# A two-phase attention and mixture-of-experts kernel on one core: lambda and bias set-up moved, the last second layers reordered, unread matmuls added on TensorE

## The chip, the core and the metric

The kernel runs on one core of one Trainium2 chip. The metric is the device time of one execution in microseconds (us); the time of the kernel before is the median of three runs. Engines are called as the profile calls them: PE is TensorE's matmul stream and PEld its weight loads, DVE is VectorE, ACT is ScalarE, POOL is GpSimd, SP is SyncE, which issues most DMAs.

## What is computed

The input is 8192 tokens of width 256. Phase 1 is a differential attention over the heads of one token (not over the sequence), with a residual:

```
x1 = x + ((attn1 - lam*attn2) * rms * ln_w + ln_b) * (1 - LAMBDA_INIT) @ Wo      # heads of layernorm(x)
lam = exp(sum(lq1*lk1)) - exp(sum(lq2*lk2)) + LAMBDA_INIT
scores = softmax(layernorm(x1) @ w_gate); top 2 of 8 experts, capacity 1024 rows each
out = x1 + sum over the 2 experts of weight * ((silu(a) * g) @ c_proj[e]),  [a, g] = row @ c_fc[e]
```

Phase 2 is the experts' part: each expert has up to 1024 rows, 256 wide, a first layer to 2 x 384 and a second layer back to 256. `ln_b` is not zero, so its contribution through Wo is a row of 256 numbers, the same for every token: the bias row.

## The kernel before

Every engine has its own program, in order, and semaphores join them.

**Phase 1** goes over 64 tiles of 128 tokens. Each engine runs steps i = 0, 1, 2, ..., and in a step it handles one stage each of several tiles. DVE in step i: `score_subtract` (L993) of tile i-1, `prob_difference` (L1012, gives w_att) of i-2, `score_products` (L972) of tile i, `prob_sum` (L1000) of i-1, `score_sum` (L979) of i, `prob_normalise` (L1005) of i-1, `score_max` (L986) of i, `scale_a` (L1020) of i-3, and every fourth tile the gating's small operations. ACT makes copies, exponentials and logarithms (xT L489, k_sb L494, x1 L570, aT_sq L552, aT_ln L557, p_ln/p_rec L543/L546). POOL multiplies attention weights with V in `head_products` (L238, one instruction of 2048 columns a tile) and issues two indirect DMAs a tile that scatter the token's row into a table in HBM sorted by expert (L419). PE in step i: `project_qk` (L762) of tile i-2, `sum_heads` (L785, 16 transposes that add up the heads) of i-6, `project_v` (L773) of i-3, `mean_squares` (L792) of i-6, `out_project` (L801 to L808) of i-7, `transpose_x` (L752) of i. `project_qk(t)` waits for DVE's products of tile t-2, `sum_heads(t)` for POOL's products of tile t.

Set-up work sits between these steps. In step 0 DVE centres the weights (L914, L918), then does `lambda_terms` (L924 to L928; it waits for the last small weight loads), then `score_products(0)`. ACT takes the exponentials of lambda in step 2 (L471). PE makes the bias row in PSUM in step 5 (L738). DVE, in step 3, splits the row into three bf16 parts whose sum is the f32 value, in nine dependent instructions of 265 columns (`bias_split`, L949 to L958), and places part j in row j of `bias_parts`. `out_project` then adds the bias with one bf16 matmul of ones by `bias_parts` (L801); the first `out_project` waits for it. The constants are made by POOL at the start; the semaphore `consts` goes to 1 when the identity matrix and a few others are ready.

At the end of phase 1 POOL issues the scatters of the last tiles one after the other. When all have landed, SP loads the first chunk of the table (`xe`, L343).

**Phase 2** goes over 16 chunks of 512 rows, two for each expert; steps are called m. In step m PE does, for j = 0, 1, 2, a third of the first layer of chunk m-1 (L872: 12 matmuls of 512 columns), after the first of them the eight transposes that take in chunk m (L863), and then the whole second layer of chunk m-2 (L883: 36 matmuls of 256 columns, for each 128 rows k nine matmuls; it waits until all three thirds j of the hidden layer are there). f32 numbers are split into a high and a low part, made by ACT and DVE (x_hi L658, x_lo L1217, silu L663, hidden L1222, h_hi L670, h_lo L1226). The second layer's result is scaled by ACT (`scale_output`, y_sb L679) and added to the output by POOL with one indirect DMA for each 128 rows (L451), four for each chunk. In step 16, and only there, the second layer of chunk 14 stands after the last third of the first layer of chunk 15:

```
def second_layer_after(m):
    return NHT - 1 if isinstance(m, int) and m == CHUNKS else 0
```

Step 17 is the second layer of chunk 15 alone.

Of the kernel before, what the change touches and what calls it, by code (L numbers as in the profile page):

```python
# [6 lines left out]
P = 128  # L7
# [38 lines left out]
def build_block(nc, x, wq, wk, wv, wo, lq1, lk1, lq2, lk2, ln_w, ln_b, w_gate, c_fc, c_proj, out):  # L46
# [11 lines left out]
    with ExitStack() as ctx:  # L58
# [27 lines left out]
        with ExitStack() as first:  # L86
# [14 lines left out]
            bias_h = [one(f"bias_h{j}", [P, E + AUX], BF16) for j in range(3)]  # L101
            bias_r = [one(f"bias_r{j}", [P, E + AUX]) for j in range(2)]
            bias_s = [one(f"bias_s{j}", [P, E + AUX]) for j in range(2)]
# [84 lines left out]
        wo_scaled = sem("wo_scaled")  # L188
# [88 lines left out]

        def second_layer_after(m):
            return NHT - 1 if isinstance(m, int) and m == CHUNKS else 0
# [82 lines left out]
        def _(pool):  # L362
# [35 lines left out]
            chain(pool.memset(g_before[0][:, :], 0.0))  # L398
            chain(pool.memset(rows[:, :, :], 0.0))
# [5 lines left out]
            pool.nop().then_inc(consts, 1)  # L405

# [17 lines left out]
            def step(i):  # L424
                if live(i - 11):
                    scatter(i - 11)
                if 0 <= i < LAST_V:
                    head_products(pool, i)

# [35 lines left out]
        def _(act):  # L465
# [135 lines left out]
            def step(i):  # L601
# [28 lines left out]
                if live(i):  # L630
                    copy_xT(i)
                if live(i - 3):
# [49 lines left out]
            def chunk_step(m, v, turn):  # L682
# [4 lines left out]
                for j, q in tiles:  # L687
# [6 lines left out]
                    if j == second_layer_after(m) and chunk_live(m, 2):  # L694
# [5 lines left out]
        def _(pe):  # L700
            pe.wait_ge(consts, 1)

# [153 lines left out]
            pe.wait_ge(slot_ready, NG)  # L856

# [29 lines left out]

            def chunk_step(m, v, turn):
                b0, b1, b2 = v % 2, (v - 1) % 2, (v - 2) % 2
                wb1, wb2 = ((v - 1) // NCH) % 2, ((v - 2) // NCH) % 2  # L890
                for j in range(NHT):
# [16 lines left out]
        def _(dve):  # L908
# [27 lines left out]

            def bias_split():

                n = 0

                def after(ins):
                    nonlocal n
                    n += 1
                    ins.then_inc(bias_chain, 1)
                    dve.wait_ge(bias_chain, n)

                dve.wait_ge(consts, 2)
                dve.wait_ge(bias_done, 1)
                after(nc.vector.tensor_copy(bias_f[:, :], bank_wo[:, 0:E + AUX]))  # L949
# [318 lines left out]
```

## Time and profile before

| | us |
|---|---|
| median of 3 runs | 696.95 (695.79 to 697.55) |
| the profiled execution | 695.95 |
| its span, first to last instruction | 694.1 |
| phase 1, to the last scatter's issue | about 0 to 453 |
| phase 2 | about 454 to 694 |
| mean granted TensorE clock | 0.969 of full |

The rows below are from that one execution. A timeline row gives the start, the time taken, the engine and line, the operation with the tile that it writes and those that it reads, the number of instructions merged in it, and in brackets how long the engine had been idle and what ended that. A granted clock of 1.00 is 2.4 GHz, 0.50 is 1.2 GHz.

### The profile page before, as it was taken

The page shows a single profiled execution, that of the slowest core. Times are in us where ns is not written, and L with a number is a line of the kernel's source. Part 1 is how long each engine was busy: PE and PEld are TensorE (multiplying, and loading weights), DVE is VectorE, ACT ScalarE, POOL GpSimd, SP SyncE. Part 2 cuts the span into 40 slices and gives each one's busy share as a digit, 9 for nine tenths or more (in the row PEclk, how much of TensorE's full clock was granted, in tenths as well). Part 3 has the DMA queues.
Part 4 walks back from the last instruction along what each step waited for, and adds up shares of the span by engine and source line. Part 5 has one row for each costly group of instructions (what it writes and reads, how often), then busy time and mean ns, then how long its engine had stood idle before and what let it go on. Part 6 is the DMA issues. An engine that isn't in the chain of part 4 may idle for free. (4 is left out here: it accounts for less than half of the span.)

```text
span 694.1 us, 12873 instructions
## 1 busy us (share of the span) xinstructions
PE 634.8 (91%) x3644; PEld 507.8 (73%) x3644; DVE 529.8 (76%) x1202; ACT 487.3 (70%) x1692; POOL 512.1 (74%) x294
## 2 busy tenths in 40 slices
PE   6889999999999999999999997049999999999990
PEld 3567777777777777777777776048898898889880
DVE  3999999999999999999999997214455456455430
ACT  3568889888988998898899888425455455465440
POOL 4446688898899889889989887734567566676534
PEclk9999999999999999999999999559999999999996
DMA  7991113223222322211201001133565664764434
GB/s 197 346 358 42 32 63 108 64 77 109 82 74 93 106 74 71 92 48 31 63 2 32 31 1 32 32 95 106 78 140 111 132 139 77 160 139 67 69 32 51
DMA packets 57836, 63.43 MB, mean 91 GB/s; under 512 B 7449, under 2 KB 53630, under 8 KB 57776
## 3 DMA queue, kind: packets, MB, share of 16 engines
q1 hardware_dynamic: 42416, 45.66, 20.6%
q0 software_dynamic: 15360, 17.08, 14.2%
q8 instruction: 24, 0.39, 0.3%
q14 instruction: 36, 0.29, 0.1%
HBM read 27.57 MB, written 43.78 MB: 103 GB/s over the span
## 5 line engine op out<-in xcount | busy, mean ns | idle before, releaser
L238 POOL TENSOR_TENSOR v_prod<-w_att,v_sb 128x2048 f32<-128x2048 f32 x62 | 233.0, 3759 | 50.4 <-DVE w_att L1012 47.2
L419 POOL DMA_INDIRECT slot_table<-rows,g_slot x128 | 129.1, 1009 | 32.0 <-issue 30.6
L451 POOL DMA_INDIRECT out_dram<-y_sb,e_tok x64 | 99.6, 1557 | 65.3 <-ACT y_sb L679 50.8
L979 DVE TENSOR_REDUCE bank_s<-qk_prod 128x128 f32<-128x2048 f32 x64 | 146.1, 2282 | 0.0
L972 DVE TENSOR_TENSOR qk_prod<-bank_qk,k_sb 128x2048 f32<-128x2048 f32 x64 | 145.8, 2279 | 0.0
L785 PEld LDWEIGHTS bank_a<-ident,v_prod 128*128 128x128 f32 x1024 | 115.5, 141 | 33.8 <-issue 30.4
L762 PE MATMUL bank_qk<-wqkv,xT 128*128 128x512 f32 x256 | 120.7, 594 | 4.7 <-DVE qk_prod L972 4.7
L785 PE MATMUL bank_a<-ident,v_prod 128*128 128x128 f32 x1024 | 122.3, 273 | 1.0 <-POOL v_prod L238 1.0
L762 PEld LDWEIGHTS bank_qk<-wqkv,xT 128*128 128x128 f32 x256 | 43.7, 190 | 36.2 <-issue 36.2
L773 PE MATMUL bank_v<-wqkv,xT 128*128 128x265 f32 x256 | 69.3, 393 | 0.0
L670 ACT CAST h_hi<-hidden 128x512 fp32r<-128x512 f32 x48 | 29.9, 622 | 55.8 <-DVE hidden L1222 55.8
L808 PE MATMUL bank_wo<-wo_s,aT_n 128*128 128x265 f32 x256 | 67.9, 387 | 0.0
L438 POOL TENSOR_TENSOR w_lo<-w,w_hi 128x1536 fp32r<-128x1536 f32 (+1 forms) x16 | 43.0, 2709 | 25.9 <-ACT w_hi L649 25.9
L1226 DVE TENSOR_TENSOR h_lo<-hidden,h_hi 128x512 fp32r<-128x512 f32 x48 | 33.5, 699 | 22.8 <-ACT h_hi L670 22.8
L773 PEld LDWEIGHTS bank_v<-wqkv,xT 128*128 128x128 f32 x256 | 43.7, 190 | 4.7
L808 PEld LDWEIGHTS bank_wo<-wo_s,aT_n 128*128 128x128 f32 x256 | 43.8, 191 | 4.2
L792 PE MATMUL bank_a<-aT_sq,head_ones 128*128 128x256 f32 x128 | 38.6, 383 | 5.3 <-ACT aT_sq L552 5.3
L580 ACT ACTIVATE rows<-x_ring,neg_mr,rstd 128x256 f32<-128x256 f32 x64 | 38.4, 600 | 5.3
L552 ACT ACTIVATE aT_sq<-bank_a 128x256 f32<-128x256 f32 x64 | 24.5, 382 | 22.2 <-PE bank_a L785 22.2
L1222 DVE TENSOR_TENSOR hidden<-silu,bank_a 128x512 f32<-128x512 f32 x24 | 16.4, 684 | 27.7 <-ACT silu L663 27.6
L1222 DVE TENSOR_TENSOR hidden<-silu,bank_qk 128x512 f32<-128x512 f32 x24 | 16.5, 687 | 25.4 <-ACT silu L663 25.2
L1212 DVE CAST e_tok<-xe 128x4 int32<-128x4 f32 x16 | 16.9, 1056 | 24.5 <-DMA out_dram<-y_sb,e_tok 24.5
(168 smaller groups left out, 1417.5 us busy)
## 6 DMA issues: line engine op xcount, KB each, us to landing
slot_table<-fill SPq DMA_DIRECT2D x8, 1056.0 KB, 13.1
xe<-slot_table SPq DMA_DIRECT2D x16, 528.0 KB, 3.7
out_dram<-x_ring SPq DMA_DIRECT2D x16, 512.0 KB, 3.0
x_ring<-in_L_attn_x_dram SPq DMA_DIRECT2D x15, 512.0 KB, 3.6
w<-in_L_ffn_c_fc_dram SPq DMA_DIRECT2D x8, 768.0 KB, 5.1
w<-in_L_ffn_c_proj_dram SPq DMA_DIRECT2D x8, 384.0 KB, 5.7
slot_table<-rows,g_slot POOLq DMA_INDIRECT x128, 2.5
out_dram<-fill SPq DMA_DIRECT2D x1, 1024.0 KB, 13.5
```

Source lines behind the costliest of these rows:

```text
L238: eng.tensor_tensor(v_prod[b][:, :, :].rearrange("p m (n e) -> p m n e", n=H), w_att[b][:, :, :].rearrange("p n m -> p m n").unsqueeze(3). ...
L419: pool.indirect_dma_start(out=table, out_offset=bass.IndirectOffsetOnAxis(ap=g_slot[g % SLOT_BUFS][:, j, k:k + 1], axis=0), in_=rows[:, r, ...
L438: pool.tensor_tensor(lo[b][:, :, :].rearrange("p k n -> p (k n)"), w[b][:, :, :].rearrange("p k n -> p (k n)"), hi[b][:, :, :].rearrange(" ...
L451: pool.indirect_dma_start(out=out, out_offset=bass.IndirectOffsetOnAxis(ap=e_tok[n % 2][:, k:k + 1], axis=0), in_=y_sb[n % 2][:, k, :], in ...
L580: nc.scalar.activation(rows[:, r, 0:E], x_ring[:, u, 0:E], ACT.Identity, bias=neg_mr[:, u:u + 1], scale=rstd[:, u:u + 1]).then_inc(xn2_rea ...
L762: last = nc.tensor.matmul(bank_qk[b][:, :, :].rearrange("p a e -> p (a e)"), xT[t % XT][:, k, :], wqkv[:, k, 0:2 * E], start=(k == 0), sto ...
L773: last = nc.tensor.matmul(bank_v[:, 0:E + AUX], xT[t % XT][:, k, :], wqkv[:, k, 2 * E:], start=(k == 0), stop=(k == 1))
L785: last = nc.tensor.matmul(bank_a[b][:, k * P:(k + 1) * P], v_prod[b][:, m, k * P:(k + 1) * P], ident[:, :], is_transpose=True, start=(m == ...
L792: nc.tensor.matmul(bank_a[b][:, E:], head_ones[:, :], aT_sq[b][:, :], start=True, stop=True).then_inc(ms_done, 1)
L808: last = nc.tensor.matmul(bank_wo[:, 0:E + AUX], aT_n[b][:, k * P:(k + 1) * P], wo_s[:, k, :], start=False, stop=(k == 1), skip_group_chec ...
L972: nc.vector.tensor_tensor(qk_prod[b][:, :].rearrange("p (n m f) -> p n m f", n=H, m=H), q4, k4, ALU.mult).then_inc(qk_multiplied, 1)
L979: nc.vector.tensor_reduce(scores[b].rearrange("p (c s) -> p s c", c=2), qk_prod[b][:, :].rearrange("p (s c d) -> p s c d", c=2, d=D), AX_X ...
```

## The change

- `lambda_terms` moves on DVE from ahead of `score_products(0)` to behind `score_sum(0)`; its exponentials move on ACT from step 2 to step 4.
- The bias row is copied from PSUM by ACT (`copy_bias`, step 5, behind `copy_xT(5)`), and the split moves from DVE to POOL, where it stands behind `head_products(0)` and so ahead of `head_products(1)`. It becomes seven instructions: the three parts are put into rows 0, 32 and 64 of `bias_parts` by copies of one partition each, the rest of which is cleared at the start.
- PE issues five matmuls of the identity by itself, 128 columns, ahead of its first wait for weights, and thirty of them between the phases, behind a wait for the scatters of tile 61. Nothing reads their result.
- In step 16 the second layer of chunk 14 stands after the first third, as in other steps. The second layer of chunk 15 is reordered: j is the outer loop, so that the parts of j = 0 and 1 need only the first two thirds of the hidden layer.

```diff
@@ gpsimd @@
+            chain(pool.memset(bias_parts[:, :], 0.0))
...
+            def bias_split():
...
+                pool.wait_ge(bias_copied, 1)
+                after(pool.tensor_copy(bias_h[0][:, :], bias_f[:, :]))
+                after(pool.tensor_tensor(bias_r[0][:, :], bias_f[:, :], bias_h[0][:, :], ALU.subtract))
+                after(pool.tensor_copy(bias_h[1][:, :], bias_r[0][:, :]))
+                after(pool.tensor_tensor(bias_r[1][:, :], bias_r[0][:, :], bias_h[1][:, :], ALU.subtract))
+                after(pool.tensor_copy(bias_parts[0:1, :], bias_h[0][0:1, :]))
+                after(pool.tensor_copy(bias_parts[32:33, :], bias_h[1][32:33, :]))
+                pool.tensor_copy(bias_parts[64:65, :], bias_r[1][64:65, :]).then_inc(bias_ready, 1)
+                pool.wait_ge(bias_ready, 1)
...
                 if 0 <= i < LAST_V:
                     head_products(pool, i)
+                if i == 0:
+                    bias_split()
@@ scalar @@
+            def copy_bias():
+                act.wait_ge(bias_done, 1)
+                nc.scalar.copy(bias_f[:, :], bank_wo[:, 0:E + AUX]).then_inc(bias_copied, 1)
...
-                if i == 2:
-                    lambda_exps()
...
                 if i == 4:
+                    lambda_exps()
                     copy_gate()
...
                     copy_xT(i)
+                if i == 5:
+                    copy_bias()
...
-                    if j == second_layer_after(m) and chunk_live(m, 2):
+                    if j == 0 and chunk_live(m, 2):
                         scale_output(m - 2, b2)
@@ tensor @@
             pe.wait_ge(consts, 1)
+            def keep_going():
+
+                nc.tensor.matmul(bank_v[:, 0:P], ident[:, :], ident[:, :], start=True, stop=True)
+
+            for _ in range(5):
+                keep_going()
...
             pe.wait_ge(slot_ready, NG)
+            pe.wait_ge(scattered[(NT - 3) % ROWS], 32 * ((NT - 3) // ROWS + 1))
+            for _ in range(30):
+                keep_going()
...
+            def last_second_layer(n, b, wb):
+
+                for j in range(NHT):
+                    past(pe, h_lo_ready, n * NHT + j)
+                    for k in range(CB):
+                        if j == 0 and k % 2 == 0:
+                            past(pe, y_scaled, n * CB + k + 1, CB)
+                        parts = ((h_lo, w2_hi), (h_hi, w2_lo), (h_hi, w2_hi))
+                        for i, (h, w) in enumerate(parts):
+                            last = nc.tensor.matmul(p2_y[k // 2][:, (k % 2) * E:(k % 2 + 1) * E], h[b][:, j, k * P:(k + 1) * P], w[wb][:, j, :],
...
+                        if j == NHT - 1 and k % 2 == 1:
+                            last.then_inc(y_done, 1)
...
-                    if j == second_layer_after(m) and chunk_live(m, 2):
-                        past(pe, h_lo_ready, (m - 2) * NHT + NHT - 1)
+                    if j == 0 and chunk_live(m, 2):
                         past(pe, w_lo_ready, expert_of(v, turn, 2) * 2 + 1)
-                        second_layer(m - 2, b2, wb2)
+                        if isinstance(m, int) and m == CHUNKS + 1:
+                            last_second_layer(m - 2, b2, wb2)
+                        else:
+                            past(pe, h_lo_ready, (m - 2) * NHT + NHT - 1)
+                            second_layer(m - 2, b2, wb2)
@@ vector @@
-            def bias_split():
...
-                if i == 3:
-                    bias_split()
                 if i == 0:
                     centre_weights()
-                    lambda_terms()
...
                 if live(i):
                     score_sum(i)
                 if i == 0:
                     numbers_of_experts()
+                    lambda_terms()
```

## Rows read from the trace of the kernel before

**Rows 1.** Busy time in one stretch of phase 1: engines, then clock, DMA share, GB/s

```profile
220.00:260.00 40.00, 40.00 (x226) 30.02 (x225) 39.89 (x105) 36.14 (x145) 35.98 (x20) 1.00 0.25 85
```

**Rows 2.** Timeline of the start, PE, ACT and DVE

```profile
4.44 3.75 PE L707 MATMUL bank_qk<-w_raw,mean_w 128*128 128x512 f32 x4 [4.44 <-DMA w_raw<-in_L_attn_Wk_dram]
...
11.68 0.38 ACT L494 ACTIVATE k_sb<-bank_qk 128x256 f32<-128x256 f32 x1 [1.35 <-PE bank_qk L762]
...
14.00 0.19 DVE L924 TENSOR_TENSOR lam_prod<-lam_in 128x32 f32<-128x32 f32 x1 [3.55 <-DMA lnwb<-in_L_attn_ln_b_dram]
...
14.33 2.28 DVE L972 TENSOR_TENSOR qk_prod<-bank_qk,k_sb 128x2048 f32<-128x2048 f32 x1
...
30.62 0.35 ACT L489 COPY xT<-bank_t 128x256 f32<-128x256 f32 x1
```

**Rows 3.** Timeline around the bias split on DVE, and PE's wait behind it

```profile
35.48 0.42 DVE L949 COPY bias_f<-bank_wo 128x265 f32<-128x265 f32 x1
...
39.97 0.28 DVE L993 TENSOR_TENSOR s_sub<-bank_s,s_max 128x128 f32<-128x128 f32 x1
...
41.00 0.70 PE L792 MATMUL bank_a<-aT_sq,head_ones 128*128 128x256 f32 x2 [3.08 <-ACT aT_sq L552]
```

**Rows 4.** Timeline between the phases: tile 61's last scatter, first chunk

```profile
447.04 0.97 POOL L419 DMA_INDIRECT slot_table<-rows,g_slot  x1 [0.30 <-issue]
...
458.43 1.09 PE L863 MATMUL bank_t<-ident,xe 128*128 128x128 f32 x4 [18.79 <-DMA xe<-slot_table]
...
461.81 1.19 PE L872 MATMUL bank_qk<-x_hi,w_lo 128*128 128x512 f32 x2 [1.45 <-ACT x_hi L658]
...
466.72 0.60 PE L863 MATMUL bank_t<-ident,xe 128*128 128x128 f32 x4
```

**Rows 5.** The chain that ended last, in order of time

```profile
452.16 2.06 DMA slot_table<-rows,g_slot
...
663.20 2.72 PE bank_qk L872 x12
...
671.04 2.16 PE bank_a L883 x18
```

**Rows 6.** Timeline of the end, chunks 14 and 15

```profile
660.52 0.60 ACT L663 ACTIVATE silu<-bank_qk 128x512 f32<-128x512 f32 x1 [0.74 <-PE bank_qk L872]
...
662.52 0.69 DVE L1226 TENSOR_TENSOR h_lo<-hidden,h_hi 128x512 fp32r<-128x512 f32 x1 [0.69 <-ACT h_hi L670]
...
668.50 0.53 PEld L883 LDWEIGHTS bank_wo<-w_hi,h_lo 128*128 128x128 f32 x3
...
672.42 1.55 POOL L451 DMA_INDIRECT out_dram<-y_sb,e_tok  x1 [9.76 <-ACT y_sb L679]
...
679.83 1.55 POOL L451 DMA_INDIRECT out_dram<-y_sb,e_tok  x1 [0.30 <-issue]
```

**Rows 7.** Stretches around PE's pauses: busy times, granted clock, DMA share, GB/s

```profile
36.00:40.00 4.00, 1.92 (x14) 1.44 (x12) 3.75 (x12) 0.16 (x1) 0.00 (x0) 1.00 1.09 335
...
434.00:436.00 2.00, 0.00 (x0) 0.00 (x0) 1.11 (x13) 1.94 (x11) 1.45 (x2) 0.89 0.27 86
...
465.00:466.00 1.00, 1.00 (x4) 0.81 (x3) 0.00 (x0) 0.00 (x0) 0.00 (x0) 0.50 0.58 207
```

**Rows 8.** POOL's elementwise groups by form: busy us, mean ns, idle before

```profile
L238 POOL TENSOR_TENSOR v_prod<-w_att,v_sb 128x2048 f32<-128x2048 f32 x62 | 233.0, 3759 | 50.4 <-DVE w_att L1012 47.2 <-ACT v_sb L530 2.0
...
L438 POOL TENSOR_TENSOR w_lo<-w,w_hi 128x1536 fp32r<-128x1536 f32 x8 | 28.1, 3507 | 25.9 <-ACT w_hi L649 25.9
L438 POOL TENSOR_TENSOR w_lo<-w,w_hi 128x768 fp32r<-128x768 f32 x8 | 15.3, 1911 | 0.0
```

**Rows 9.** Timeline of tile 0 from POOL's products to PE, and project_qk(5)

```profile
25.56 3.75 POOL L238 TENSOR_TENSOR v_prod<-w_att,v_sb 128x2048 f32<-128x2048 f32 x1 [16.94 <-DVE w_att L1012]
...
32.25 0.59 PE L792 MATMUL bank_a<-aT_sq,head_ones 128*128 128x256 f32 x2
...
33.32 1.95 PE L762 MATMUL bank_qk<-wqkv,xT 128*128 128x512 f32 x4 [0.26 <-DVE qk_prod L972]
```

More of the change, by code:

```diff
@@ L100, in build_block @@
             bias_f = one("bias_f", [P, E + AUX])
-            bias_h = [one(f"bias_h{j}", [P, E + AUX], BF16) for j in range(3)]
+            bias_h = [one(f"bias_h{j}", [P, E + AUX], BF16) for j in range(2)]
             bias_r = [one(f"bias_r{j}", [P, E + AUX]) for j in range(2)]
-            bias_s = [one(f"bias_s{j}", [P, E + AUX]) for j in range(2)]
             bias_parts = one("bias_parts", [P, E + AUX], BF16)
@@ L187, in build_block @@
             sem(n) for n in "wo_transposed woT_copied gate_folded gate_copied bias_done bias_ready".split())
-        wo_scaled = sem("wo_scaled")
+        wo_scaled, bias_copied = sem("wo_scaled"), sem("bias_copied")
         x_transposed, xT_copied, qk_done, v_done, k_copied, aux_copied, v_copied = (
@@ L276, in chunk_live @@
             return not isinstance(m, int) or 0 <= m - lag < CHUNKS
-        def second_layer_after(m):
-            return NHT - 1 if isinstance(m, int) and m == CHUNKS else 0
         def expert_of(v, turn, lag):
@@ L405, in _, with after @@
             pool.nop().then_inc(consts, 1)
+            def bias_split():
+                n = 0
+                def after(ins):
+                    nonlocal n
+                    n += 1
+                    ins.then_inc(bias_chain, 1)
+                    pool.wait_ge(bias_chain, n)
+                pool.wait_ge(bias_copied, 1)
[7 more added lines that the diff above has]
+                pool.wait_ge(bias_ready, 1)
             def scatter(t):
@@ L886, in second_layer @@
                         last.then_inc(y_done, 1)
+            def last_second_layer(n, b, wb):
[7 more added lines that the diff above has]
+                            last = nc.tensor.matmul(p2_y[k // 2][:, (k % 2) * E:(k % 2 + 1) * E], h[b][:, j, k * P:(k + 1) * P], w[wb][:, j, :],
+                                                    start=(j == 0 and k % 2 == 0 and i == 0), stop=(j == NHT - 1 and i == len(parts) - 1),
+                                                    skip_group_check=True)
+                        if j == NHT - 1 and k % 2 == 1:
+                            last.then_inc(y_done, 1)
             def chunk_step(m, v, turn):
@@ L935, in lambda_difference @@
                 dve.wait_ge(lam_chain, 4)
-            def bias_split():
[L939 to L949, printed above, removed]
-                after(nc.vector.tensor_copy(bias_h[0][:, :], bias_f[:, :]))
-                after(nc.vector.tensor_tensor(bias_r[0][:, :], bias_f[:, :], bias_h[0][:, :], ALU.subtract))
-                after(nc.vector.tensor_copy(bias_h[1][:, :], bias_r[0][:, :]))
-                after(nc.vector.tensor_tensor(bias_r[1][:, :], bias_r[0][:, :], bias_h[1][:, :], ALU.subtract))
-                after(nc.vector.tensor_copy(bias_h[2][:, :], bias_r[1][:, :]))
-                after(nc.vector.tensor_scalar(bias_s[0][:, :], bias_h[0][:, :], ident[:, 0:1], None, ALU.mult))
-                after(nc.vector.scalar_tensor_tensor(out=bias_s[1][:, :], in0=bias_h[1][:, :], scalar=ident[:, 1:2], in1=bias_s[0][:, :],
-                                                     op0=ALU.mult, op1=ALU.add))
-                nc.vector.scalar_tensor_tensor(out=bias_parts[:, :], in0=bias_h[2][:, :], scalar=ident[:, 2:3], in1=bias_s[1][:, :],
-                                               op0=ALU.mult, op1=ALU.add).then_inc(bias_ready, 1)
             def numbers_of_experts():
```

## The prediction

> **What bounds the kernel now.** I read the busy times by stretch first, then the timelines of the start, of the change between the phases and of the end. In the middle of phase 1 both PE and DVE work without a pause, 40.00 and 39.89 of 40 us [rows 1]; POOL and ACT have some 4 us left. So phase 1 is as long as the one of the two whose unbroken run begins too late. DVE's run begins at 14.33 [rows 2]. PE's begins at 41.00, after 3.08 us of waiting [rows 3]: DVE split the bias from 35.48, so its s_sub came only at 39.97, ACT's exponential of it and the squares behind it stood in the queue, and `mean_squares(1)` waited for these. From there on PE issues the same instructions whatever the change does, so **phase 1 ends earlier by as much as `mean_squares(1)` does, and no more**. What DVE saves beyond that it gives back waiting for PE.
>
> Between the phases POOL's scatters lead, then one load; the granted clock has fallen to half, and PE's first third of a layer takes 461.81 to 466.72, 4.91 us [rows 4], where one at full clock takes 2.72 [rows 5]. At the end POOL leads: the four output scatters of chunk 15 start at 679.83 [rows 6] and all behind them is fixed.
>
> **Lambda.** DVE waited 3.55 us for the small loads although k_sb was done at 11.68 + 0.38 = 12.06. It can begin the products at 12.1. The four small instructions, 14.33 - 14.00 = 0.33, return behind `score_sum(0)`, where the loads have long landed. Gain for DVE 14.33 - 12.1 - 0.33 = 1.9 us [rows 2]. The exponentials in ACT's step 4 are one small instruction in a queue that waits for DVE: nothing, and if that cover is gone, its own 0.2 us (an estimate from DVE's 0.19 for an instruction of like size).
>
> **Five matmuls at the start.** PE's four passes of 512 columns run at 0.85 us each, 3.75 with the last one's tail [rows 2], the half clock. In rows 4 PE worked from 461.81 on, and the clock was still 0.50 in 465 to 466 [rows 7] and full soon after, say 4.4 us after the work began. An identity matmul of 128 columns is two passes of a quarter of 0.85, so five take 2.1 us, from about 2.1 (when the identity is made) to 4.3: done when the weights come at 4.44 [rows 2]. If the clock then rises at 2.1 + 4.4 = 6.5, the last one and a half passes take half as long: 0.65 us. Bounds: 0 (it rises as before) to 1.7 (all four passes at full clock). DVE's total lead is then 2.5 us.
>
> **Bias split.** DVE loses its nine instructions, about 3.75 us, and the pause of PE that they caused. But POOL gets seven, in front of `head_products(1)`. The copy on ACT stands behind xT(5), which was at 30.62 [rows 2] and hangs on DVE's sums, so it comes 2.5 us earlier: copy 28.4 to 28.75, POOL starts at 28.85. Prices: a subtract of two tensors takes (3507 - 1911)/768 = 2.08 ns a column and 0.32 us fixed [rows 8], so 265 columns 0.87; by v_prod's 1.84 ns a column alone it would be 0.49. I take 0.85 twice, since L438 is the same operation. A copy has one input instead of two: half of a subtract, 0.43, between 0.25 and 0.87, five times. Between dependent instructions 0.1 (between 0 and the 0.3 that POOL stood ahead of a scatter [rows 6]), seven times. Sum 1.7 + 2.15 + 0.7 = 4.55, between 2.2 and 8.2. The split ends at 33.4, and `head_products(1)` can only start then. From the start of tile 0's products to its mean_squares 32.25 - 25.56 = 6.7 us passed [rows 9], so `mean_squares(1)` comes at 40.1 against 41.00: **gain 0.9 us** (between 3.2 and -2.7). What POOL adds takes back most of what DVE is freed of. The Trainium skill speaks against such a move ("GPSIMD Engine Reference", section 4.1: elementwise work on tiles belongs on VectorE, GpSimd being about twice as slow with two inputs); by its factor on the 0.42 us that DVE takes here for 265 columns [rows 3] a subtract would be 0.84, so the sum would stay.
>
> **PE's pause grows.** `project_qk(5)` began at 33.32 and took 1.95 [rows 9]; 2.5 us earlier it ends at 32.8. `sum_heads(1)` can start once POOL's 3.75 us are over, so at 37.2. PE stands still for 4.4 us, where it stood for 3.08 at a clock that stayed 1.00 [rows 3, 7]. At 434 to 436 the clock fell within 2 us of PE's stop [rows 7]. So I expect that it falls here, to 1.2 GHz, and that PE works about 4.4 us at half speed before it rises: 2.2 us lost (0.7 to 3.4, as the moment falls), all on the path. Phase 1 comes out at 0.9 - 2.2 = **1.3 us longer**. The Trainium skill ("TensorE: Matmul & The Clock Gate", part 1) says that what the chip watches runs free of the kernel; by that the moment of each fall and rise differs from run to run.
>
> **Thirty matmuls between the phases.** Tile 61's last scatter is issued at 447.04 [rows 4]; tile 63's took 2.26 us from issue to SP's next load (452.16 to 454.42, its 2.06 in rows 5), so PE starts at 449.3. Sixty passes: 4.4 us at half clock make 21 of 0.21, the other 39 take 0.107 each, 4.2 us. They end at 457.9, half a us before the chunk is there at 458.43. Then the eight transposes take half the time, ACT and DVE get their input earlier, and the first layer starts 0.8 us earlier (the copies between stay; 0.5 to 1.0); the first third takes 2.72 instead of 4.91, 2.2 less [rows 4, 5]. Gain **3.0 us** (1.5 to 3.3). PE is on the path from there to 675, so nothing hides it.
>
> **The end.** h_lo of chunk 14 is there at 663.21 [rows 6]; its second layer starts at 663.3 instead of 668.50 and takes 4.4. It ends at 667.7; two thirds of 2.72 follow, to 673.1. From the end of a third to h_lo took 663.21 - 660.52 + 0.4 = 3.1 us, so h_lo of the last is there at 676.2, and the parts of j = 0 and 1, 24 matmuls of 0.12 [rows 5], are done at 676.0. The first pair of row blocks needs 12 less than the whole: 6 matmuls, 0.7 us, to 677.0. Before, the first scatter came 672.42 - 668.50 - 2.16 = 1.76 us after such a pair, so it starts at 678.75 instead of 679.83. Chunk 14's four, 1.85 us each, are over by 675.5, even if they start at 668. Gain **1.1 us** (0.3 to 1.5); the chain silu, hidden, h_hi, h_lo is late next.
>
> **Sum.** 695.95 + 1.3 - 3.0 - 1.1 = 693.15 for the profiled execution. The median of the runs is 1.0 above it, so 694.15, I say 694.1. POOL's clearing of 265 columns at the start delays only fills that are queued behind SP's loads until 12.7: nothing, or 0.2 if SP were waiting.
>
> **Rivals.** (a) The clock stays up in PE's pause at 33 to 37, as it did over 3.08 us: phase 1 gains 0.9, in all 5.0 less, 691.9. (b) The split is near its lower end, 2.2 to 3 us, the pause is shorter than before and the clock stays: phase 1 gains up to 3.2, in all 7.3 less, 689.7. For it: v_prod's rate; against: L438. (c) The thirty do not do what they are for: they are done at 457.9 or earlier, PE stands again until 458.43 and from 459.3 to 461.0, and the clock is at half when the first layer starts. Then the 3.0 falls away: 697.1. For it: the fall within 2 us at 434; against: no fall in 3.08 us at 38 to 41. (d) Slower: the thirty end late. If weight load and matmul do not overlap, a pass costs some 0.25 us, PE is busy until 449.3 + 4.4 + 39 x 0.25 = 463.5, and the chunk waits 5.1 us: 694.1 + 5.1 = 699.2. It decides from 0.25 us a pass on; below 458.43 nothing is lost. Against it: the second layer's 18 matmuls of 256 columns take 2.16 us with a weight load for each [rows 5], so such a load hides behind 0.12 us.
>
> **How the numbers follow.** The forecast has 0.5, with a range of its own of 692.3 to 696.2; (a) 0.25, (b) 0.07, (c) 0.12, (d) 0.06. A measurement of this kernel can tell about 0.3% or 2.1 us from no change: faster is below 694.9, slower above 699.0. Faster: about four fifths of the forecast, all of (a) and (b), 0.72. Same: the rest of it and most of (c), 0.22. Slower 0.06. The range 690.2 to 697.3 leaves out (b), (d) and the tails.
>
> **What would show it.** DVE's first products at about 11.5; POOL's seven instructions between 28.9 and 33.4 and head_products(1) behind them; PE idle some 4.4 us, a clock of 0.50 in part of 35 to 42, mean_squares(1) near 40 to 42; in phase 2, shifted by phase 1, PE's thirty ending before the chunk lands, clock 1.00 at the first layer, its first third 2.7 us; the last four scatters 1.1 us closer to it. Wrong would be: DVE waiting nowhere and phase 1 shorter by over 4 us (then PE is not the pacer), a clock of 1.00 throughout 33 to 42, or the chunk's transposes waiting for PE's own queue.

## The result and the profile after

The kernel after takes **692.39 us** (median of 4 runs, 691.81 to 693.75) beside 697.20 of the kernel before in the same comparison: ratio 0.9936, 95% interval 0.9916 to 0.9956. The profiled execution took 693.75 us, its span is 692.0 us: it is the longest of its four, while the profiled one of before is among its kernel's shortest. So the two traces differ by 2.1 us where the medians differ by 4.8, and sizes below are checked against medians of parts and against the traces of the other runs.

The start, in the timeline of the kernel after (start, duration, engine, line; in brackets the idle time ahead and what ended it):

```profile
1.96 2.50 PE L729 MATMUL bank_v<-ident 128*128 128x128 f32 x10 [1.96 <-POOLq L376]
...
11.54 0.38 ACT L517 ACTIVATE k_sb<-bank_qk 128x256 f32<-128x256 f32 x1 [1.67 <-PE bank_qk L793]
...
11.96 2.29 DVE L1000 TENSOR_TENSOR qk_prod<-bank_qk,k_sb 128x2048 f32<-128x2048 f32 x1 [1.88 <-ACT k_sb L517]
...
16.56 0.18 DVE L976 TENSOR_TENSOR lam_prod<-lam_in 128x32 f32<-128x32 f32 x1
```

DVE no longer waits for the small loads: its products begin at 11.96 instead of 14.33 [rows 2], and lambda's instructions stand behind the first sums. k_sb itself came only 0.14 us earlier (11.68 before).

The split and what follows it, same timeline (POOL, DVE, PE):

```profile
28.77 0.38 ACT L507 COPY bias_f<-bank_wo 128x265 f32<-128x265 f32 x1
...
29.21 0.41 POOL L415 CAST bias_h<-bias_f 128x265 bf16<-128x265 f32 x1 [2.02 <-ACT bias_f L507]
...
29.70 0.69 POOL L416 TENSOR_TENSOR bias_r<-bias_f,bias_h 128x265 f32<-128x265 f32 x1
...
32.63 0.41 POOL L421 CAST bias_parts<-bias_r 1x265 bf16<-1x265 f32 x1
...
33.12 3.73 POOL L237 TENSOR_TENSOR v_prod<-w_att,v_sb 128x2048 f32<-128x2048 f32 x1
...
33.38 3.62 DVE L1033 TENSOR_TENSOR p_norm<-probs,p_rec 128x128 f32<-128x128 f32 x1
...
36.90 3.28 PEld L816 LDWEIGHTS bank_a<-ident,v_prod 128*128 128x128 f32 x16 [4.55 <-POOL v_prod L237]
36.90 3.68 PE L816 MATMUL bank_a<-ident,v_prod 128*128 128x128 f32 x16 [3.72 <-POOL v_prod L237]
...
42.14 0.60 PE L823 MATMUL bank_a<-aT_sq,head_ones 128*128 128x256 f32 x2
```

The seven instructions last from 29.21 to 33.04, `head_products(1)` comes behind them, PE waits 3.72 us for it, and `mean_squares(1)` is at 42.14 (41.00 in [rows 3]). The row to dwell on is DVE's `p_norm`: 3.62 us for an instruction whose mean in the kernel before is 0.277 us. It has no wait ahead of it; the 3.3 us are inside its own duration, and it ends 0.15 us after POOL's `v_prod`.

PE in stretches (length, busy time, number of instructions, granted clock, DMA share, GB/s):

```profile
8.00:35.31 27.31, 21.82 (x93) 1.00 0.96 294
35.31:42.14 6.83, 5.24 (x21) 0.50 1.09 336
42.14:438.08 395.94, 387.92 (x2245) 1.00 0.20 69
438.08:455.15 17.07, 5.29 (x27) 0.50 0.04 3
455.15:680.40 225.25, 219.13 (x1319) 1.00 0.53 106
```

The clock falls in PE's pause, to 1.2 GHz, and is back at 2.4 GHz only at 42.14. Between the phases it rises at 455.15 and stays up. The timeline there:

```profile
450.23 9.28 PE L729 MATMUL bank_v<-ident 128*128 128x128 f32 x60 [9.57 <-DMA slot_table<-rows,g_slot]
459.38 0.66 PE L897 MATMUL bank_t<-ident,xe 128*128 128x128 f32 x4
...
462.08 0.70 PE L906 MATMUL bank_qk<-x_hi,w_lo 128*128 128x512 f32 x2 [1.61 <-ACT x_hi L682]
...
464.91 0.27 PE L897 MATMUL bank_t<-ident,xe 128*128 128x128 f32 x1
```

The last scatter of phase 1 starts at 453.16, 1.00 later than in [rows 5]. From there to the first layer it is 8.92 us instead of 9.65, and the first third takes 2.83 instead of 4.91 [rows 4]. The end:

```profile
664.70 0.84 ACT L703 ACTIVATE y_sb<-bank_wo,e_w 128x256 f32<-128x256 f32 x2
...
665.96 1.55 POOL L470 DMA_INDIRECT out_dram<-y_sb,e_tok  x1 [5.08 <-ACT y_sb L703]
...
675.41 0.84 ACT L703 ACTIVATE y_sb<-bank_wo,e_w 128x256 f32<-128x256 f32 x2 [1.88 <-PE bank_wo L931]
...
676.14 0.84 ACT L703 ACTIVATE y_sb<-bank_a,e_w 128x256 f32<-128x256 f32 x2
...
677.35 1.55 POOL L470 DMA_INDIRECT out_dram<-y_sb,e_tok  x1 [4.30 <-ACT y_sb L703]
```

The last four scatters start at 677.35 instead of 679.83 [rows 6]. Phase 1 (+1.00) and the middle (-0.73, -2.08) explain 1.81 of the 2.48, so in this pair of traces the new end is worth 0.67. Chunk 14's first scatter stands 1.26 us behind the start of its `y_sb`, the last chunk's 1.94. Of the 2.48 the span keeps 2.1: from the first of these four scatters to the end of the span it is 14.65 us here and 14.26 before. It is 14.55 to 14.72 in seven of the eight traces with the split on POOL, 14.30 in the eighth, and 14.26 to 14.34 in the six others; no row shows why.

### The profile page after: what moved, and what is told of

Its sections match the earlier page's. It is cut to its first block and busy times, and to the rows that moved or that the text cites. A ratio compares the mean times of both kernels' runs of the same rounds, so it can differ in the third digit from the quotient of the medians.

```text
span 692.0 us, 13005 instructions
## 1 busy us (share of the span) xinstructions
PE 645.4 (93%) x3714; PEld 519.0 (75%) x3714; DVE 530.6 (77%) x1193; ACT 487.3 (70%) x1693; POOL 515.7 (75%) x302
## 5 line engine op out<-in xcount | busy, mean ns | idle before, releaser
L816 PEld LDWEIGHTS bank_a<-ident,v_prod 128*128 128x128 f32 x1024 | 117.0, 142 | 37.8 <-issue 30.7
L816 PE MATMUL bank_a<-ident,v_prod 128*128 128x128 f32 x1024 | 124.0, 275 | 4.7 <-POOL v_prod L237 4.7
```

The costliest lines, as they stand in the source:

```text
L816: last = nc.tensor.matmul(bank_a[b][:, k * P:(k + 1) * P], v_prod[b][:, m, k * P:(k + 1) * P], ident[:, :], is_transpose=True, start=(m == ...
```

## The experiments

All times are medians, each beside the kernel before in the same comparison.

| run | us | before | ratio to before, 95% |
| --- | --- | --- | --- |
| the kernel after | 692.39 | 697.20 | 0.9936 (0.9916 to 0.9956) |
| only_split | 698.37 | 697.48 | 1.0012 (0.9998 to 1.0026) |
| only_lambda | 695.96 | 697.48 | 0.9981 (0.9970 to 0.9993) |
| only_end | 696.14 | 697.48 | 0.9985 (0.9972 to 0.9998) |
| only_five | 697.07 | 696.92 | 1.0007 (0.9994 to 1.0020) |
| only_thirty | 695.89 | 696.92 | 0.9977 (0.9965 to 0.9990) |
| five_and_thirty | 693.87 | 697.28 | 0.9945 (0.9926 to 0.9964) |
| phase_one | 695.70 | 697.28 | 0.9982 (0.9966 to 0.9997) |
| without_thirty | 695.23 | 697.28 | 0.9972 (0.9959 to 0.9985) |
| warm_pause | 690.78 | 696.92 | 0.9909 (0.9891 to 0.9927) |
| split_behind_1 | 687.79 | 697.48 | 0.9861 (0.9841 to 0.9880) |
| handshake | 688.36 | 696.92 | 0.9874 (0.9853 to 0.9895) |
| pause_until_issued | 687.41 (one run) | 697.28 | |

One number of the traces sorts the runs of phase 1: the time from the start of DVE's first products to the start of the last scatter. "Clock" is what the granted clock did in PE's pause ahead of `mean_squares(1)`.

| run | first products | last scatter | between | clock in the pause |
| --- | --- | --- | --- | --- |
| before | 14.33 | 452.16 | 437.83 | stays |
| only_end | 13.43 | 451.27 | 437.84 | stays |
| only_thirty | 13.33 | 451.14 | 437.81 | stays |
| only_five | 13.43 | 452.86 | 439.43 | falls |
| only_lambda | 11.75 | 451.31 | 439.56 | falls |
| five_and_thirty | 13.40 | 454.13 | 440.73 | falls |
| only_split | 13.75 | 453.76 | 440.01 | falls |
| phase_one | 11.36 | 451.70 | 440.34 | falls |
| the kernel after | 11.96 | 453.16 | 441.20 | falls |
| without_thirty | 11.89 | 453.18 | 441.29 | falls |
| warm_pause | 11.57 | 450.23 | 438.66 | stays, pause filled |
| handshake | 11.69 | 447.58 | 435.89 | no pause |
| pause_until_issued | 10.99 | 446.87 | 435.88 | no pause |
| split_behind_1 | 10.85 | 446.71 | 435.86 | no pause |

In the three kernels of the top rows phase 1 has the same instructions, and the times between agree to 0.03 us: their last scatters differ only by when the first products start, and this by when the small loads come that lambda waits for (14.00 in before, 13.00 to 13.42 in the five other traces with lambda in its old place). With nearly the same pause of 3.1 us (3.08 in before and only_thirty, 3.09 in only_lambda and five_and_thirty) the clock stayed up in two executions and fell in two.

**Where the split stands in POOL's queue.** The kernel after, with the split one step later, behind `head_products(1)`:

```
-                if i == 0:
+                if i == 1:
                     bias_split()
```

> The changed kernel with POOL's bias split one step later, behind head_products(1) instead of ahead of it; everything else as changed. Theory P (PE paces phase 1 from mean_squares(1) on, and POOL's seven instructions held it up): head_products(1) starts near 29.0 instead of 33.1, mean_squares(1) comes near 35.6 instead of 42.1, PE's pause ahead of sum_heads(1) is under 2 us and the granted clock stays 1.00 through 30 to 45; head_products(2) is now the late one, so mean_squares(2) comes near 43.4 instead of 48.4 and phase 1 ends about 5 us earlier: 687.4 us, between 686 and 690. Rival D (DVE paces phase 1, and POOL's place in the queue is hidden): within 1 us of the changed kernel's 692.4.

It takes 687.79 us, in the range, 4.6 less than the kernel after (4.9 when each is taken from the before of its own comparison), and beats both kernels. POOL and DVE in its timeline:

```profile
27.83 3.75 POOL L237 TENSOR_TENSOR v_prod<-w_att,v_sb 128x2048 f32<-128x2048 f32 x1 [1.75 <-DVE w_att L1040]
...
32.02 0.69 POOL L416 TENSOR_TENSOR bias_r<-bias_f,bias_h 128x265 f32<-128x265 f32 x1
...
32.29 0.56 DVE L1033 TENSOR_TENSOR p_norm<-probs,p_rec 128x128 f32<-128x128 f32 x1
...
35.43 3.75 POOL L237 TENSOR_TENSOR v_prod<-w_att,v_sb 128x2048 f32<-128x2048 f32 x1
...
38.54 0.78 DVE L1033 TENSOR_TENSOR p_norm<-probs,p_rec 128x128 f32<-128x128 f32 x1
```

The products of tile 1 start at 27.83 instead of 33.12 (1.11 of this because DVE's first products came earlier in this execution, 10.85 and 11.96), PE has no pause of a microsecond there, `mean_squares(1)` is at 35.72, as expected, and `mean_squares(2)` at 41.96, earlier than the 43.4 expected. From the first products to the last scatter it is 5.34 us less than in the kernel after. And DVE is held far less: by 0.28 us behind a subtract of the split (32.02 + 0.69 = 32.71, `p_norm` ends at 32.85) and by 0.5 us behind the next products (39.18 and 39.32). In each of these rows `p_norm`, which has two inputs in SBUF, ends 0.14 or 0.15 us after POOL's instruction, whatever time it had begun. In the kernel after, 3.34 us of DVE go that way. That DVE and POOL exclude each other here is read from these rows; no run took the overlap away by itself. The Trainium skill states it ("SBUF — State Buffer", section "SBUF: two separate sides"): VectorE with two SBUF inputs and a GpSimd operation that reads SBUF share one pair of ports, whoever starts first has it for the whole instruction, and the other stands. The rows agree.

**The same split without lambda's lead.** The kernel before with the split's hunks of the diff alone (`bias_split` on POOL, `copy_bias` on ACT, the clearing of `bias_parts`); the first call is DVE's, the second POOL's:

```
-                if i == 3:
-                    bias_split()
+                if i == 0:
+                    bias_split()
```

> The kernel before with the move of the bias split to POOL alone (copy on ACT, split behind head_products(0)). Theory P: without DVE's lead from the lambda move, the copy comes near 31.0, the split ends near 35.3, mean_squares(1) comes near 42 if the clock holds and near 44 if it falls, against 41.00 before: 698.2 to 700.4 us, slower than before by 1 to 3. Rival D: DVE is rid of 3.75 us and paces, so about 693.5.

698.37, at the low end of the range: no gain from freeing DVE, a small loss if any (the interval includes none). Its trace has the same hold (`p_norm` 3.61 us at 34.90), a clock that falls at 38.97, and `mean_squares(1)` at 42.79. DVE is freed of 3.75 us of split and then stands for 3.3.

**Lambda alone.** The kernel before with these hunks:

```
                 if i == 0:
                     centre_weights()
-                    lambda_terms()
...
                 if i == 0:
                     numbers_of_experts()
+                    lambda_terms()
...
-                if i == 2:
-                    lambda_exps()
...
                 if i == 4:
+                    lambda_exps()
                     copy_gate()
```

> The kernel before with lambda_terms behind score_sum(0) and its exponentials in ACT's step 4, alone. Theory P: DVE's run starts at 12.1, comes back to 2.0 us of lead after the four small instructions, and since in this kernel mean_squares(1) hangs on DVE's bias split, it comes at 39.0 instead of 41.00: 695.2 us. Rival Z (the lambda wait was hidden, the lead is given back within the first tiles): 697.2, no change. Rival D expects 695.2 as well.

695.96, 0.8 us above what was expected, with `mean_squares(1)` at 38.69, 2.3 earlier than in [rows 3]. Its clock fell at 38.25, and that gave back 1.4 us: 439.56 from the first products to the last scatter, less 0.33 for lambda's own instructions, against 437.83. The gain was also priced on an execution whose loads came late. In the five other traces with lambda in its old place the first products start at 13.33 to 13.75 and not at 14.33, and the same sum gives 0.9 to 1.3 us instead of 1.9.

**All edits of phase 1 together.** The kernel after less the thirty, `last_second_layer` and the moved second layer of chunk 14:

> The edits of the first phase together (five matmuls, lambda, split in GpSimd's queue), without the thirty and the new end. By the sum of the parts alone: 697.0 + 0.0 - 1.2 + 1.2 = 697.0. By the prediction (lead of VectorE pays the split's wait, 0.9 gained, then 2.2 lost by the clock) 698.3. Theory H (the lead pays the wait): the wait of TensorE for v_prod is 3.7 us in both, but VectorE stands 2 us further on by then, so part of the split's 1.2 us isn't charged twice: 696.0 to 696.5, and 692.4 + 2.8 + 1.1 = 696.3 by the whole kernel less its other two parts.

695.70, somewhat better than all three figures. Lambda and split alone give 0.9981 and 1.0012, so together they would give 0.9993; measured is 0.9982. The intervals overlap, so that the lead pays part of the split's wait is not shown.

**PE's pause filled.** The kernel after with 14 more unread matmuls ahead of the sum over the heads of tile 1:

```
+                if i == 7:
+                    keep_warm(14)
                 if live(i - 6):
                     sum_heads(i - 6)
```

> The kernel after with 14 more unread matmuls on TensorE where it waited 3.72 us for v_prod of tile 1 (ahead of the sum over the heads). Theory C (the clock): the pause itself costs what it costs, and the fall of the granted clock from 35.31 to 42.14 us comes on top, about 2.2 us of matmuls at 0.50; with the pause filled the clock stays 1.00 from 30 to 45 us and the mean squares of tile 1 come at 39.6 to 40.1 instead of 42.14: 692.4 - 2.0 = 690.4. Rival D (the wait): phase 1 moves only as much as v_prod does, and VectorE carries the path behind it, so a slow TensorE there hides beside it: mean squares of tile 1 may come earlier, but the last scatter stays at 453.2 within 0.4: 692.0 to 692.4. If fourteen run past the end of the wait, they delay the sum by under 0.8 us.

690.78: 1.6 us less than the kernel after. A stretch of PE, and three rows of its timeline:

```profile
30.00:45.00 15.00, 14.14 (x89) 1.00 1.09 342
```

```profile
32.99 3.62 DVE L1039 TENSOR_TENSOR p_norm<-probs,p_rec 128x128 f32<-128x128 f32 x1
...
39.22 0.59 PE L827 MATMUL bank_a<-aT_sq,head_ones 128*128 128x256 f32 x2
...
450.23 0.97 POOL L436 DMA_INDIRECT slot_table<-rows,g_slot  x1 [0.30 <-issue]
```

The clock stays at 1.00, and `mean_squares(1)` and the last scatter both come 2.9 us earlier, 0.4 of it because the start was quicker in this execution (first products at 11.57, not 11.96). DVE is held just as long. So 2.5 us is what the fall cost in the profiled execution (441.20 against 438.66), and 1.6 in the median. In phase_one, which has the same pause, the clock was low for 3.4 us instead of 6.8 and the time between is 1.7 above 438.66; so the cost follows how long the clock is down, and that differs between executions. From here to split_behind_1 (another 3.0 us) remain POOL's later products and DVE's 3.3 us.

**The five matmuls alone.** The kernel before with five calls of the unread matmul ahead of the first wait for weights:

```
+            for _ in range(5):
+                keep_going()
```

> The kernel before with the five matmuls ahead of the first weights alone. Prediction's term: 0.65 us, because the clock rises earlier (696.5). In the profile of the kernel after, the rise came at 8.0 instead of 8.89 us and the first scores' input was only 0.07 us earlier on VectorE, and qk_means took as long as before. Theory now: VectorE in the first stretch doesn't wait for TensorE at that clock, so they are worth 0 to 0.1: 697.1 to 697.2. Rival (the prediction's term): 696.5, with wqkv on VectorE 0.5 us or more earlier than 8.31.

697.07: nothing. But this kernel cannot show what the five are worth, since lambda is in its old place, and DVE waits for its loads long after k_sb is there (11.11 + 0.38 = 11.49):

```profile
13.10 0.19 DVE L931 TENSOR_TENSOR lam_prod<-lam_in 128x32 f32<-128x32 f32 x1 [3.67 <-DMA lnwb<-in_L_attn_ln_b_dram]
```

The rival's sign did come: `wqkv` on DVE starts at 7.60, 0.71 earlier than in before, in an execution where the clock rose at 6.66 (8.24 and 8.00 in the kernel after, 8.31 and 8.89 in before). All traces together suggest that the five help a little and unevenly: `k_sb` starts at 11.34 to 11.68 in the five without them, mean 11.53, and at 10.43 to 11.55 in the nine with them, mean 11.12. The five do not settle when the clock rises.

**The thirty alone.** The kernel before with two lines of the change:

```
+            pe.wait_ge(scattered[(NT - 3) % ROWS], 32 * ((NT - 3) // ROWS + 1))
+            for _ in range(30):
+                keep_going()
```

> The kernel before with the thirty matmuls during the last scatters alone. Theory: in the kernel after, the last scatter of phase 1 to the first first-layer instruction fell from 9.65 to 8.92 us (0.73) and the first third of that layer from 4.91 to 2.83 us (2.08), so this edit by itself is worth 2.8 us; 697.2 - 2.8 = 694.4, and the profile shows a granted clock that rises near 455 us and then stays at 1.00, with the first third at 2.8 us. Rival: the rise is taken back elsewhere (the clock falls again in the chunks, or the chunk waits for the last of the thirty matmuls), the gain is under 1 us: 696.5. By the parts that ran (the rearranged split with its queue +1.2, lambda with the five matmuls -1.2, the end -1.1, together -1.1) and the whole change (-4.8), the thirty should be worth 3.7 if all add up: 693.5. Between 693.5 and 694.8 for the theory.

695.89: a gain of 1.0 us, not 2.8. The rival has it right in size, and only in part in cause. The profiled execution (696.04) does not show even that gain: from the last scatter of phase 1 to the first of the last four scatters it has 228.69 us, where before has 227.67. The DMA queues of this run from 451 to 455 us (busy tenths and GB/s in 40 slices of 0.1 us, then the queues):

```profile
DMA  0000110000000000011000500000000000000000
GB/s 0 0 0 0 3 3 0 0 0 0 0 0 0 0 0 0 0 3 3 0 0 0 164 0 0 0 0 0 0 0 0 0 0 0 0 0 0 0 0 0
...
q8 instruction: 1, 0.02, 1.4%
...
slot_table<-rows,g_slot POOLq DMA_INDIRECT x1, 4.2
```

One packet of 16 KB of code runs from 453.25, among the packets of the last scatter, which was issued at 451.14: 45 of its 48 packets ran by 452.9, the other three at 454.1, behind the code. That scatter takes 4.2 us to land, the others about 2.1. SP's load of the first chunk is issued at 455.52, 4.38 us after the scatter instead of 2.26, PE is done with its thirty at 456.9 and stands for 2.51 us, and the clock falls once more:

```profile
451.87:462.11 10.24, 6.12 (x54) 1.00 0.33 107
462.11:465.52 3.41, 3.41 (x8) 0.50 0.47 117
```

In the seven traces without the thirty no packet of code runs between 446 and 460 us; each of the seven with them has one there, of 16 KB. Here it comes 5.04 us behind the start of the thirty (448.21); in the kernel after it comes 2.62 us behind it, ahead of the last scatter's packets. Five more matmuls stand in front of it there, ten passes; ten passes at half clock take about 2.3 us (an estimate; the ten at the start of the kernel after took 2.50 with the last one's tail), about what separates 5.04 from 2.62. This gives a sharp forecast: the five, worth nothing alone, should make the thirty worth their full price.

> The kernel before with the five matmuls at the start and the thirty during the last scatters: two edits that took 697.07 and 695.89 by themselves, beside 696.92. With the thirty alone a fetch of 16 KB of code stood at 453.25 us, 5.04 us behind the start of the thirty, where the last scatter's own packets ran, and that scatter took 4.2 us to land instead of 2.1. In the kernel after the fetch stood 2.62 us behind their start, ahead of the last scatter's packets. Theory F: the five put ten passes ahead in the code, the fetch comes some ten passes (at 0.23 us each, 2.3 us) earlier, as in the kernel after, and misses the last scatter: load of the first chunk 2.3 us behind the last scatter instead of 4.4, the time about 697.0 - 2.8 = 694.2, though by the sum of the two alone it would be 696.0. Rival G: 696.0, with or without the fetch in the way.

**693.87**, 3.4 us below before, though the two edits alone gained -0.15 and 1.03. Of the two ratios alone the product is 0.998, outside the interval of this run. Its DMA queues from 453 to 457 us:

```profile
DMA  0110000050000011000000000002000000000000
...
q8 instruction: 1, 0.02, 1.4%
...
slot_table<-rows,g_slot POOLq DMA_INDIRECT x2, 2.5
```

The packet stands at 453.8, 2.6 us behind the start of the thirty (451.18), between the packets of two scatters; the load is issued 2.25 us behind the last scatter (454.13), and the clock stays 1.00 from 455.50. From the last scatter to the last four it is 224.75 us, against 228.69 with the thirty alone and 227.10 to 228.26 in the five traces with the old end and no thirty.

The kernel after less the three lines of the thirty:

> The kernel after without the thirty matmuls during the last scatters. They alone gained 1.0 us on the kernel before, where 2.8 was read from the traces of before and after. Theory F (a fetch in the way): the thirty matmuls of the kernel after are worth the 2.8 us that its trace shows, so without them it takes 692.4 + 2.8 = 695.2; what spoiled them alone was a code fetch that met the last scatter. Rival G (the rise is worth little in most executions): they are worth 1.0 here too, 693.4. In the profile: first third of the first layer 4.9 us again, granted clock 0.50 there.

695.23, as theory F has it: in place, the thirty are worth 2.84 us by the medians of two comparisons (2.5 by their ratios to before).

**The end alone.** The kernel before with `last_second_layer` (j outermost) and chunk 14's second layer ahead of the last chunk's later thirds:

```
+                        if isinstance(m, int) and m == CHUNKS + 1:
+                            last_second_layer(m - 2, b2, wb2)
+                        else:
...
-                    if j == second_layer_after(m) and chunk_live(m, 2):
+                    if j == 0 and chunk_live(m, 2):
```

> The kernel before with the two edits at the end alone: the second layer of chunk 14 behind the first third, and that of chunk 15 with j outermost. As recorded in the prediction 1.1 us less (696.1); by the changed kernel's trace, in which the first of the last four scatters stands 1.94 us behind its y_sb instead of the 1.23 to 1.34 of the other chunks, 0.7 less (696.5). If that 1.94 is a chance of one execution, the scatter here comes 1.3 behind its y_sb.

696.14: a gain of 1.3 us, but its ratio allows 0.1 to 2.0, so this run cannot tell the 1.1 of the prediction from the 0.7 of the trace. In place the end is worth 0.5 (phase_one 695.70, without_thirty 695.23). Its last chunk has the same 1.94 us from `y_sb` (676.19) to the first scatter (678.13).

**Why 1.94 and not 1.26.** In the traces before these two runs the late scatter stood 0.37 to 0.43 us behind the end of ACT's row of `y_sb`, which scales two blocks in chunk 14 and four in chunk 15, and this suggested that ACT holds POOL. Two kernels, both with the split behind tile 1, take ACT's row apart. In the first (shown) ACT stops after the first block until POOL has passed its wait; in the second the `nop` stands behind the scatter:

```
                 for k in range(CB):
                     pool.wait_ge(y_scaled, n * CB + k + 1)
+                    if n == CHUNKS - 1 and k == 0:
+                        pool.nop().then_inc(first_seen, 1)
                     pool.indirect_dma_start(
...
+                    if isinstance(n, int) and n == CHUNKS - 1 and k == 0:
+                        act.wait_ge(first_seen, 1)
```

> The kernel after with the split behind the scatters of tile 1 (the one that took 687.79), and now ScalarE stops after the first scaled block of the last chunk until GpSimd has passed its wait for it. Theory B (the burst): the first scatter of the last chunk starts only when ScalarE's run of scaled blocks has ended, 0.36 to 0.42 us after it: with four in a run it stood 1.94 us behind its own block, with two 1.23 to 1.34 in the other chunks. With a pause after the first it stands about 0.85 behind it, and the four scatters, which follow each other at 1.85 us, end about 1.1 us earlier: 687.8 - 1.0 = 686.8. Rival Q (GpSimd's own time): the 1.94 us are what a scatter needs from its wait on, whatever ScalarE does; then nothing is gained, the scatter stays 1.9 behind its block: 687.8 or, if the pause pushes the second block past the second scatter, up to 688.2. The profile tells: scatter minus end of first block, 0.8 to 0.9 by B, 1.9 by Q.

> As the run called handshake, but now ScalarE scales the second to fourth block of the last chunk only when GpSimd has issued the first scatter. In that run the first scatter stood 1.96 us behind the start of the first scaled block though GpSimd had passed its wait, and 0.22 us behind the end of ScalarE's other three. Theory B2 (GpSimd's start waits for a ScalarE that works): with ScalarE still, the scatter starts 1.23 to 1.34 us behind the start of its block, as in the other chunks. Rival Q2 (it is in GpSimd's own code or queue at that place): 1.9 us again. The time itself: 688.4 plus up to 0.6, since the second scatter now waits for its block.

In the second, ACT's wait is the same and the `nop` stands here:

```
                     ).then_inc(y_added[n % 2], 16)
+                    if n == CHUNKS - 1 and k == 0:
+                        pool.nop().then_inc(first_seen, 1)
```

The first took 688.36, the second 687.41 (one run), beside 687.79 of split_behind_1: no gain in the first, and none that one run can show in the second. The second's timeline:

```profile
669.32 0.47 ACT L705 ACTIVATE y_sb<-bank_wo,e_w 128x256 f32<-128x256 f32 x1 [1.88 <-PE bank_wo L935]
...
671.09 0.47 ACT L705 ACTIVATE y_sb<-bank_wo,e_w 128x256 f32<-128x256 f32 x1 [1.29 <-POOLq L475]
671.26 1.55 POOL L470 DMA_INDIRECT out_dram<-y_sb,e_tok  x1 [4.30 <-issue]
```

ACT stands still from 669.79 to 671.09 (POOL's queue has passed the scatter by then, 0.17 us ahead of the scatter's own row), and the scatter still starts 1.94 us behind its block. **The theory of ACT's row is dead**: the first scatter of the last chunk follows its block by 1.94 to 1.96 us in all seven traces with the new end, whatever ACT does. Why POOL needs 0.7 us more there than for chunk 14 stays open; no packet of code was in flight at that time.

## Why the prediction was right, and where it was not

The forecast was 694.1 with a range of 690.2 to 697.3; the kernel takes 692.4. By its steps:

- **Phase 1 moves as `mean_squares` moves.** Held: +1.14 at tile 1 and +1.00 at the last scatter in the profiled execution; -5.39 at `mean_squares(2)` (47.35 and 41.96) and -5.45 at the end of phase 1 in split_behind_1; +1.93 and +1.97 in five_and_thirty. Tile 2 is the safer mark, since the clock can still fall behind tile 1, as in only_lambda.
- **Lambda.** The 1.9 us for DVE came (14.33 to 11.96 is 2.37, less 0.33 for lambda's own, 2.04), against an execution of before whose loads came late; against the others it is 0.9 to 1.3. The 0.65 us for the five matmuls did not: k_sb gained 0.14. The step that failed is "the clock then rises at 6.5": it rose at 8.00 in this execution, and between 5.49 and 8.35 in the nine traces with the five.
- **Bias split**, forecast 4.55 us, measured 3.9 to the start of the products (29.21 to 33.12): the subtract takes 0.69 and not 0.85, the copies 0.40 to 0.41 as priced, the gaps some 0.07 and not 0.1. It starts at 29.21, not 28.85, so the products start at 33.12, not 33.4. The prediction's estimate by the Trainium skill ("GPSIMD Engine Reference", section 4.1), 0.84 for the subtract, was as high as my own; the measurement decides, and it is 0.69.
- **PE's pause and the clock.** 3.72 us of pause instead of 4.4; the clock fell in the profiled execution, as forecast against rival (a), for 6.8 us. The cost of the fall was put at 2.2 us; warm_pause shows 2.5 for this execution and 1.6 in the median.
- **What was missed: DVE's hold.** The prediction let DVE run on while POOL multiplied. It stood for 3.34 us, almost what it had been freed of. In this kernel PE waited for the same products anyway, so that the sum didn't suffer is likely and not shown. What the prediction also did not try is the split's place in POOL's queue: one step later is worth 4.6 us, of which the fill of the pause accounts for 1.6; how the rest divides between POOL's products and DVE's hold is open.
- **Thirty matmuls**, forecast 3.0 us: 2.81 in the trace, 2.84 by the run without them. They ended level with the arrival of the chunk (459.5 and 459.38), not half a microsecond before it, so rival (d) came within sight. Rival (c) was right for the edit by itself, for a reason nobody had named.
- **The end**, forecast 1.1, measured 0.67 in the pair of traces, 0.5 in place by medians, 1.3 (0.1 to 2.0) alone. The pair of row blocks was done when forecast (675.1 where the forecast, moved by 1.81, has 675.2). The step that failed is "1.76 us after such a pair": it was 2.2. The hop was read from chunk 14, and from `y_sb` to the scatter the last chunk takes 0.7 us more.

**The total.** For the profiled execution the forecast was 693.15 and it took 693.75. Its parts, +1.3, -3.0 and -1.1, came as +1.00, -2.81 and -0.67, and 0.37 us were lost behind the start of the last scatters: small misses, partly cancelling. The median gained 4.8 us and not 2.9, though (697.20 and 692.39, against 696.95 and 694.1), and 692.4 is at the lower edge of the forecast's own 692.3 to 696.2, nearer to the 691.9 of rival (a), whose condition the profiled execution refutes. That the time still lies in the range is partly luck.

Most of what was missed lies in phase 1: the profiled execution lost 1.0 us there, but the runs of phase_one gained 1.6 in the median. The step behind it is that the forecast charged a fall of the clock to the kernel after alone. It started from an execution of before in which the clock stayed up in PE's pause. In only_five and five_and_thirty, whose phase 1 differs from before's only by the five matmuls, the clock fell there, for 3.4 and 6.8 us, and the time from the first products to the last scatter grew by 1.6 and 2.9. The profiled execution of before has a mean granted clock of 0.969; of the 75 executions of it in the three later comparisons five have that, and 70 have less, down to 0.961. How often the low stretch lies in this pause no view shows, so how the 1.6 divides stays open.

## What to carry to other kernels

Work that is moved to GpSimd can also delay VectorE where VectorE then meets GpSimd with two operands from SBUF; before choosing the place in the queue, look for VectorE instructions whose duration, not whose wait, has grown. An edit that adds instructions can move a later fetch of code out of the way of a transfer or into it: here two edits were worth 0 and 1.0 us alone and 3.4 together. Where a stage runs with the clock down after a pause, fill the pause and time the filling, and look once at a kernel with the filling alone and once without it in place. And before a sum is started from one trace of the kernel before, compare that trace with others of the same code: here the one chosen had its loads 0.6 to 1.0 us later and its clock up where other executions had it down.

## What was unexpected of the hardware

- With a 16 KB packet of code among its packets a scatter took 4.2 us to land instead of 2.1 (only_thirty); three of its 48 packets ran behind the code.
- VectorE's `p_norm`, 0.28 us elsewhere, took 3.61 to 3.62 us beside GpSimd's products in all five kernels with the split ahead of `head_products(1)` (the kernel after, warm_pause, only_split, phase_one, without_thirty), with no wait shown ahead of it.
- The clock's rise at the start lay between 5.49 and 8.35 us in kernels with the same five matmuls, and its first fall came between 25.97 and 39.07 us, or not at all ahead of 50 us. With the same pause of 3.1 us in PE it stayed up in two executions and fell in two; a fall in the pause goes with 1.4 to 2.9 us more of phase 1.
- A copy on one partition costs GpSimd as much as on 128: 0.40 and 0.41 us for 265 columns.
